# A buffer of its own for the low parts of left over edge rows in a one-core graph layer on Trainium2

## The reference: one graph layer

```python
for r in range(weight.shape[0]):
    mask = (edge_type == r).astype(x.dtype)
    sums = jax.ops.segment_sum(msgs * mask[:, None], dst, num_segments=n)
    cnt = jax.ops.segment_sum(mask, dst, num_segments=n)
    mean = sums / jnp.maximum(cnt, 1.0)[:, None]
    out = out + mean @ weight[r]
...
z = jnp.concatenate([u, x], axis=1) @ w_gate + b_gate
h = jnp.tanh(u) * z + x * (1.0 - z)
```

## Time and profile before

| what | value |
|---|---|
| median of 3 runs | 1711.09 us (1710.4 to 1714.0) |
| the profiled execution's own time | 1710.35 us |
| its span, first to last instruction | 1708.5 us |
| TensorE busy | 1594.3 us, 93% of the span |
| mean granted TensorE clock | 0.976 of full speed |

### The profile page before, as it was taken

The page is one execution under the profiler, slowest core; times in us unless marked ns, Lnnn a source line. Parts: engine busy times, 40 slices in busy tenths (PEclk is TensorE's granted clock), DMA queues, the critical chain, the costliest instruction groups (busy, mean ns, idle before and its releaser), DMA issues.

```text
span 1708.5 us, 19085 instructions
## 1 busy us (share of the span) xinstructions
PE 1594.3 (93%) x7188; PEld 1276.0 (75%) x7188; DVE 892.7 (52%) x1324; ACT 393.9 (23%) x581; POOL 784.3 (46%) x672
## 2 busy tenths in 40 slices
PE   4999999999999999999999999999899959977988
PEld 4987777666667678888788787877777748866887
DVE  6534222334331420002887888785567737777885
ACT  3321111221122112222222222222211122232220
POOL 4426676656564135545545554654655641210110
PEclk8999999999999999999999999999999979988999
DMA  4422232322232222226778777867987864540001
GB/s 154 139 97 83 77 94 86 102 84 84 85 92 96 75 82 93 87 83 213 254 237 279 242 261 258 272 220 246 332 284 259 277 227 150 183 136 1 38 38 47
DMA packets 120458, 262.47 MB, mean 154 GB/s; under 512 B 23451, under 2 KB 37010, under 8 KB 120360
## 3 DMA queue, kind: packets, MB, share of 16 engines
q1 hardware_dynamic: 48568, 109.34, 18.9%
q0 software_dynamic: 33056, 83.02, 16.0%
q10 hardware_dynamic: 38736, 68.83, 10.8%
HBM read 193.33 MB, written 80.06 MB: 160 GB/s over the span
## 4 chain that ended last, share of the span: by engine, by line
PE 62%; DVE 19%; DMA 9%; issue 5%; ACT 3%; POOL 2%; ACTq 0%; SPq 0%; POOLq 0%; DVEq 0%
PE ps L1749 45%; DMA source_rows<-relation_rows,row_list 7%; PE ps L1988 5%; PE ps L1852 3%; DVE u_sum L1506 3%; PE ps L2020 2%; PE ps L1872 2%; DVE source_rows L1490 1%; PE ps L1832 1%; PE ps L2038 1%; ACT source_rows_hi L2163 1%; PE ps L1864 1%; DMA u_sum<-u_rows 1%; POOL WL L829 1%; DVE wq_rows L559 1%
## 5 line engine op out<-in xcount | busy, mean ns | idle before, releaser
L1749 PE MATMUL ps<-WH,XTH 128*128 128x512 f32 (+1 forms) x1680 | 670.9, 399 | 0.0
L1749 PE MATMUL ps<-WL,XTH 128*128 128x512 f32 (+1 forms) x1680 | 653.1, 389 | 0.0
L1749 PE MATMUL ps<-WH,XTL 128*128 128x512 f32 (+1 forms) x1680 | 653.0, 389 | 0.0
L1749 PEld LDWEIGHTS ps<-WH,XTH 128*128 128x128 f32 x1680 | 318.1, 189 | 81.9 <-issue 22.5
L829 POOL TENSOR_TENSOR WL<-RAW,WH 128x512 fp32r<-128x512 f32 (+1 forms) x184 | 239.3, 1304 | 304.4 <-ACT WH L2098 302.2
L1749 PEld LDWEIGHTS ps<-WH,XTL 128*128 128x128 f32 x1680 | 317.1, 189 | 64.5
L1749 PEld LDWEIGHTS ps<-WL,XTH 128*128 128x128 f32 x1680 | 317.5, 189 | 60.3 <-issue 2.4
L887 POOL DMA_INDIRECT source_rows<-relation_rows,row_list x180 | 222.2, 1234 | 264.6 <-PE ps L1872 134.5
L2120 ACT ACTIVATE EV<-ps 128x512 f32<-128x512 f32 x180 | 107.3, 596 | 610.9 <-PE ps L1749 541.1
L908 POOL DMA_INDIRECT edge_lists<-edge_words x160 | 197.0, 1231 | 46.3 <-issue 42.2
L1506 DVE SCALAR_TENSOR_TENSOR u_sum<-source_rows,weight_list,u_sum 128x1024 f32<-128x1024 f32 x120 | 168.4, 1404 | 74.6 <-DMA source_rows<-relation_rows,row_list 64.5
(11 more groups left out here) (301 smaller groups left out, 1515.9 us busy)
## 6 DMA issues: line engine op xcount, KB each, us to landing
relation_rows<-EV ACTq DMA_DIRECT2D x160, 256.0 KB, 2.1
RAW<-in_L_gnn_weight SPq DMA_DIRECT2D x128, 256.0 KB, 2.7
u_rows<-u_sum SPq DMA_DIRECT2D x20, 512.0 KB, 5.1
RAW<-in_L_gnn_w_gate SPq DMA_DIRECT2D x32, 256.0 KB, 4.6
mix_rows<-mix_rows_out ACTq DMA_DIRECT2D x10, 512.0 KB, 2.6
root_rows<-EV ACTq DMA_DIRECT2D x20, 256.0 KB, 4.3
u_sum<-u_rows SPq DMA_DIRECT2D x10, 512.0 KB, 7.3
bias_rows<-root_rows SPq DMA_DIRECT2D x10, 512.0 KB, 7.0
```

The source lines that it names most:

```text
L1749: mm = t_.matmul(ps[:, bank, 0:w], a[:, t, k, :], b[:, s, k, 0:w], start=(k == 0 and j == 0), stop=(k == KT - 1 and j == 2))
```

## The change

The low part of a left over item is no longer written over the gathered rows in their slot, but into one new buffer `OLO` (`source_rows_lo`, 128 x 1024). It takes SBUF space that is also `edge_words`'. TensorE reads the low part there. The gather that reuses a left over item's slot waits for `oh_lo` (VectorE has made the low part) where it waited for `agg_used` (TensorE has summed it). Since `OLO` is one buffer, VectorE now waits for the left over item before to be summed, ahead of the one-hot matrix; it waited for the fourth before.

```diff
+        OLO, = stage_tensors(("source_rows_lo", [P, D], F32R))
...
                 if m.index >= RING:
                     old = ITEMS[m.index - RING]
-                    pool.wait_ge(agg_used if old.over else plane_done,
+                    pool.wait_ge(oh_lo if old.over else plane_done,
                                  old.count + 1 + (FIRST if old.over else 0))
...
             def left_over(m):
 
-                if m.count >= 4:
-                    dve.wait_ge(agg_used, FIRST + m.count - 3)
+                dve.wait_ge(agg_used, FIRST + m.count)
                 v.tensor_scalar(S1H[:, m.count % 4, :], iota1[:], key_list[:, m.count:m.count + 1], None,
                                 ALU.is_equal)
                 dve.wait_ge(oh_hi, FIRST + m.count + 1)
-                rows_ = XG[:, m.index % RING, :]
-                v.scalar_tensor_tensor(rows_, rows_.bitcast(F32), weight_list[:, m.column:m.column + 1],
+                v.scalar_tensor_tensor(OLO[:], XG[:, m.index % RING, :].bitcast(F32), weight_list[:, m.column:m.column + 1],
                                        OHI[:].bitcast(F32), ALU.mult, ALU.subtract).then_inc(oh_lo, 1)
...
-            def sum_rows(slot, one_hot, bank, first, last):
+            def sum_rows(low, one_hot, bank, first, last):
 
-                for j, part in enumerate((OHI[:], XG[:, slot, :])):
+                for j, part in enumerate((OHI[:], low)):
...
-                sum_rows(m.index % RING, m.count % 4, agg_bank(m.sum), m.part == 0,
+                sum_rows(OLO[:], m.count % 4, agg_bank(m.sum), m.part == 0,
                          m.part == OVER[m.group] - 1).then_inc(agg_used, 1)
```

More of the change, by code:

```diff
@@ L1890, in aggregate_round @@
                 pe.wait_ge(oh_lo, NCH * rd + q + 1)
-                sum_rows(q % RING, q % 4, agg_bank(i), c == 0, c == GCB[g] - 1).then_inc(agg_used, 1)
+                sum_rows(XG[:, q % RING, :], q % 4, agg_bank(i), c == 0, c == GCB[g] - 1).then_inc(agg_used, 1)
             QUERY_PLACES = [(1, 0), (1, 3), (1, 6), (2, 1)]
```

## The result

The changed kernel took 1698.49 us in the median of 6 runs (1696.7 to 1703.11), the kernel before 1711.42 us (1710.04 to 1714.19) beside it; the ratio is 0.9925, with a 95% interval of 0.9909 to 0.9942. The profiled execution took 1701.06 us. The forecast was 1684 us, 27 us off; the medians are 12.9 us apart and the two profiled spans 9.3 us (the profiled execution of the changed kernel lies 2.6 us above its median). The sign was right and the range held the time; the size was off by a factor of two.

What follows compares the result with a forecast made beforehand. TensorE, busy 1594.3 of 1708.5 us, was taken as the bound. Winning 12 (stage one), 14 (stage two) and 1.5 us behind, together 27.5 off 1710.35, gave 1682.9; 0.7 more for the median, rounded to 1684 us; range 1672 to 1700.

Steps and rivals of the forecast that it cites:

- 12 of 14.4 us: Stage one: of 14.4 us lost against a stretch without stalls, 12 us would be won (bounds 8 and 14.4).
- 14 of 22.9 us: Stage two: of 22.9 us lost against a stretch without stalls, 14 us would be won (bounds 6 and 22.9).
- The stall goes, with 0.6 us to spare: Stage one's first stall, 3.22 us at 839.21: low part over at 835.4, 3.8 us sooner, before TensorE comes at 835.99.
- it and the two plane slots' gathers behind it move too, and don't hold up the one at 798.5: Before the first stall: the gather at 795.96 and two behind it move sooner, letting that at 802.32 start at 798.5.
- What may stay is VectorE's: Stage one: whatever of the 14.4 us lost isn't won (12 forecast, at least 8) would be due to VectorE.
- The worked stall: Stage two, 1193.99 us: gathers at 1169.71 and 1176.05 go about 7.6 and 3.8 us sooner; the 1.49 us stall goes.
- The turn fits in the median but not at long landings: Stage two: seven items' slot reuse takes 18.4 us against TensorE's 19.2 at median landings, but 24.0 at 10.3 us landings.
- the ring isn't the limit, VectorE is, 82%: Stage one: four gather slots need 25.6 us a tile against TensorE's 35.9; VectorE, busy 294.32 of 359.4 us, limits.
- The rival that transfers bind stage two: Stage two: sooner gathers only queue up and landings grow, so some 2 us are won there; 1697 us, chance 0.18.
- The rival that GpSimd and VectorE collide: Gathers starting right after low parts: gather issue and VectorE's instructions lengthen each other, 13 us lost; 1724 us, chance 0.04.
- VectorE's new wait and the other tile: VectorE's wait for the previous sum, hidden under ScalarE's high part, and writing the low part elsewhere: each costs 0.
- Behind the stages: After stage two: sooner gathers pull in the last gate product's move and store; 1.5 us won (0 to 3.8).

Runs made afterwards that it cites:

- p1: Changed kernel's new buffer and VectorE wait, but the next gather still waits for TensorE's sum as in the kernel before; 1710.74 us, ratio 0.9979.
- p13: Kernel before, late release kept, with 18 of 24 weight quantization blocks done before step 117 and the rest spread wide; 1698.07 us, ratio 0.9915.
- p14: Changed kernel, but from step 117 GpSimd makes the next weights' low part for 16 of 512 columns only (output not the reference's); 1683.93 us, ratio 0.9817.
- p3: Changed kernel with a fifth gather slot, one-hot matrices cut from four buffers to two; 1685.17 us, ratio 0.9836.
- p9: Changed kernel with 18 of 24 weight quantization blocks before step 117 and the last six spread over steps 126 to 164; 1691.92 us, ratio 0.9882.

## Why the prediction was right about the sign and wrong about the size

- **The mechanism** (a slot free at the low part, gathers sooner, TensorE's waits shorter) is shown: p1 takes the release away and most of the gain is gone.
- **The step that failed is the size of what the stages win**, the terms "12 of 14.4 us" and "14 of 22.9 us" of the sum; they won 6.0 and 4.5. Both are below the lower bounds of 8 and 6 as well.
- **Stage one.** "The stall goes, with 0.6 us to spare" rests on a lead of 3.8 us, and that failed at the gather: "it and the two plane slots' gathers behind it move too, and don't hold up the one at 798.5". They did. The first of them waited for its plane until 794.71, L830 with 1.30 us and the second stood behind it, and the gather came 1.9 us sooner from the stage's start. The chain took another 0.4 us, and 1.5 us were left against a stall of 3.22. The other stalls were worked out one by one too, with TensorE's arrival as it was; it moves with every stall that goes, and at 910.54 us a stall came that the trace before doesn't have (4.2 us with its slower steps). "What may stay is VectorE's" had the right name and a bound that was too small. p13 shows that the release isn't even needed there once the blocks are elsewhere. p14 shows that with the release the blocks may stay if nothing holds them; the old release without the holding wasn't run.
- **Stage two.** The worked stall went, by gathers 7.6 and 3.8 us sooner, as forecast. "The turn fits in the median but not at long landings" was right too, and two thirds was too much to hope from it: 4.5 of 22.9 us is one fifth. A turn that fits by 19.2 - 18.4 = 0.8 us doesn't last through landings of up to 10.2 us. GpSimd's wait for planes, which grew by 41.6 us, took over from its wait for sums. TensorE's idle time there is 204.50 - 192.26 = 12.2 us, not 3 to 8; in stage one it is 5.1 us, not under 3.
- **In stage one "the ring isn't the limit, VectorE is, 82%"** is half right. A fifth slot takes 8.4 to 3.8 us there (p3), since slots also carry gathers across VectorE's late spells; but a lighter VectorE alone takes it to 0.6 (p9, p14) or nothing (p13).
- **The rival that transfers bind stage two** is refuted by p3: 300 GB/s and a share of 0.85 against 285 and 0.83, with landings 0.4 us longer in the median. It gave 1697 us, nearest to the measured 1698.49, for a reason that doesn't hold.
- **The rival that GpSimd and VectorE collide** named the right pair and the wrong instruction. The low part's mean went from 1568 to 1622 ns, the gather's issue from 1234 to 1237; what holds VectorE isn't the gather's issue, which p14 keeps, but the low part of the weights, and it had done so before as well, so the change pays no more for it in all (60.6 and 60.2 us), only at other places. The Trainium skill (SBUF — State Buffer, "SBUF: two separate sides") says that a VectorE instruction with two SBUF inputs and a GpSimd instruction that reads SBUF take a shared port pair exclusively, so that one blocks the other. The trace agrees that such pairs hold VectorE (L560 and L1489 beside L830).
- **VectorE's new wait and the other tile** cost nothing that can be seen: p1 isn't slower than before, and p14's low parts take 1285 ns in the median with at most 1405. The changed kernel's median is 1284 ns, as forecast.
- **Behind the stages** the forecast was 1.5 us won. From the end of stage two to the moment at which TensorE resumed after the last of three idle spells it took 34.7 us (1354.8 to 1389.46), before 34.9 (1366.0 to 1400.91): 0.2 us won. The last gate product's store moved by as much as the stages (over at 1366.29 + 7.77 = 1374.06, before at 1385.16), and TensorE resumed 11.4 us sooner. 2.1 us of these are given back later: the span is 9.3 us shorter. The first 19 us after TensorE resumed, of the changed kernel and then of the kernel before:

```profile
1389.45:1408.60 19.15, 19.14 (x76) 0.84 0.00 1
```

```profile
1400.90:1420.00 19.10, 19.09 (x82) 0.91 0.02 3
```

The granted clock is 0.84 of full speed against 0.91, so for some 6 us of the stretch it is at the lower of its two levels, 1.2 GHz, against 3.4 us before (worked out as twice what is missing to 1, times the stretch). The three idle spells ahead of it, with short work between them, were 5.62, 5.82 and 4.72 us in the changed kernel and 6.51, 4.79 and 6.11 us before. Six matmuls fewer are some 1.4 us. Why the clock came back later is open.

## What to carry to other kernels

When a wait goes, follow the whole queue behind it and not only the instruction that is freed: here the freed gather still stood behind a plane's gather and an instruction of 1.30 us, and half of the lead was gone before it started. An instruction that has become longer in the trace of after is a suspect, not yet the cause; a run in which it is short again tells. Judge the stalls of one engine together and not one by one, since each that goes brings the engine sooner to all later ones, and take the spread of one instruction's durations (here 0.53 and 2.40 us) as a question with a price before giving a figure for what can be won. Before spending a buffer on a sooner release, price the same buffer as one more slot.

## What the hardware showed that I had not expected

- A GpSimd subtraction of 128 x 512 (1.30 us) lengthens the VectorE instruction beside it by up to 1.9 us, more than it takes itself, and also one that had begun first: L560 at 809.24 would be over at 809.77 by its usual 0.53 us, the GpSimd instruction begins at 809.94, and L560 ends at 811.64. GpSimd's times in a profile are rough, so this order is what the profile shows and no more. One-input instructions are held too (L552, 0.34 to 1.85 us). In the two stages this was 60.2 us of VectorE's time, and taking it away (p14) took the ratio to the kernel before from 0.9925 to 0.9817 (0.9781 to 0.9853), more than the whole change had brought; p14's GpSimd is also less busy, and that share isn't separated.
- The same width as a copy takes GpSimd 0.63 us in the median and holds VectorE for 14.1 us in all, about a fifth.
